# Edge aggregation of a graph layer: landing buffers filled one stage earlier, and remainder columns formed on VectorE

## The reference

```python
xl = (x @ Wl).reshape(n, H, D)
xr = (x @ Wr).reshape(n, H, D)
msg = xl[src] + xr[dst]
act = jnp.where(msg > 0, msg, NEG_SLOPE * msg)
e = jnp.einsum('ehd,hd->eh', act, att)
m = jax.ops.segment_max(e, dst, num_segments=n)
p = jnp.exp(e - m[dst])
denom = jax.ops.segment_sum(p, dst, num_segments=n)
alpha = p / (denom[dst] + 1e-16)
out = jax.ops.segment_sum(alpha[..., None] * xl[src], dst, num_segments=n)
return out.reshape(n, HID) @ W_up
```

## Time and profile before

| | |
|---|---|
| median of 3 runs | 1188.15 us (1183.03 to 1191.4) |
| the profiled execution | 1185.71 us, its span 1184.0 us |
| VectorE busy | 906.6 us (77%) |
| TensorE busy | 984.3 us (83%) |
| ScalarE busy | 603.7 us (51%) |
| GpSimd busy | 398.1 us (34%) |
| maxima / first seven groups / rest of aggregation / finish | from 603.9 / 652.7 / 686.0 / 921.6 us |

### The profile page before, as it was taken

How to read it: one execution, slowest core, us unless ns; L and a number is a source line. 1 busy time by engine, 2 the same in 40 slices (tenths; PEclk the granted TensorE clock), 3 DMA queues, 4 the chain that set the end, 5 groups by cost and what they waited for, 6 DMA issues and landing times. The chain is left out here.

```text
span 1184.0 us, 16374 instructions
## 1 busy us (share of the span) xinstructions
PE 984.3 (83%) x5021; PEld 793.5 (67%) x5021; DVE 906.6 (77%) x1499; ACT 603.7 (51%) x1356; POOL 398.1 (34%) x393
## 2 busy tenths in 40 slices
PE   0588399999999999999954779999997889999934
PEld 0475289999999999999931567777776344444412
DVE  3698177877888887887775679999995399887892
ACT  0243256665766666666633367777765224323411
POOL 0211477777777677777501000000001000000000
PEclk9899599999999999999988889999998899999966
DMA  4489588898898888888731776777764223422222
GB/s 150 120 208 154 165 250 265 279 263 262 243 296 269 272 249 263 276 260 263 236 107 53 251 237 207 242 235 211 222 200 140 65 92 93 98 70 72 50 35 35
DMA packets 106320, 220.76 MB, mean 186 GB/s; under 512 B 22658, under 2 KB 55003, under 8 KB 106127
## 3 DMA queue, kind: packets, MB, share of 16 engines
q1 hardware_dynamic: 83503, 152.48, 38.9%
q0 software_dynamic: 19904, 56.35, 21.7%
q10 hardware_dynamic: 2832, 10.89, 3.1%
HBM read 157.22 MB, written 73.01 MB: 194 GB/s over the span
## 5 line engine op out<-in xcount | busy, mean ns | idle before, releaser
L880 POOL DMA_INDIRECT score_gath<-xl_rows,misc x324 | 345.6, 1067 | 108.4 <-issue 95.5
L920 PE MATMUL score_ps_m<-x_hi,score_w_hi 128*128 128x416 f32 (+1 forms) x576 | 208.8, 362 | 0.4 <-DVE score_w_lo L1073 0.4
L1535 PE MATMUL agg_ps_o<-agg_gath,agg_hot 128*125 128x256 f32 x648 | 186.2, 424 | 24.6 <-DVE agg_hot L1651 24.1
L921 PE MATMUL score_ps_m<-x_lo,score_w_hi 128*128 128x416 f32 (+1 forms) x576 | 204.1, 354 | 0.0
L922 PE MATMUL score_ps_m<-x_hi,score_w_lo 128*128 128x416 f32 (+1 forms) x576 | 203.6, 353 | 0.0
L1594 ACT ACTIVATE agg_gath<-agg_gath,prob 128x64 f32<-128x64 f32 x648 | 158.4, 338 | 26.5 <-DMA agg_gath<-edge_rows 26.5
L1054 DVE TENSOR_TENSOR score_zb<-score_gath,score_ps_x 128x1024 f32<-128x1024 f32 x81 | 98.7, 1219 | 74.1 <-PE score_ps_x L903 71.6
L1535 PEld LDWEIGHTS agg_ps_o<-agg_gath,agg_hot 128*125 128x125 f32 x648 | 100.3, 192 | 59.5 <-issue 51.9
L975 ACT ACTIVATE score_mask_t<-score_local_bc,score_neg_iota 125x512 fp32r<-125x512 bf16 x81 | 58.3, 719 | 122.9 <-DMA score_local_bc<-local_rows 122.9
L903 PE MATMUL score_ps_x<-parts,score_mask_t 125*128 x648 | 93.8, 288 | 32.6 <-ACT score_mask_t L977 32.4
L1537 PE MATMUL agg_ps_o<-ext,agg_hot 128*125 128x18 f32 x324 | 118.8, 367 | 0.0
(11 more groups left out here) (320 smaller groups left out, 1654.6 us busy)
## 6 DMA issues: line engine op xcount, KB each, us to landing
edge_rows<-score_gath SPq DMA_DIRECT2D x81, 520.0 KB, 4.1
agg_gath<-edge_rows SPq DMA_DIRECT2D x81, 520.0 KB, 3.7
score_local_bc<-local_rows SPq DMA_DIRECT2D x40, 250.0 KB
score_gath<-xl_rows,misc POOLq DMA_INDIRECT x324, 4.6
x_rows<-in_x SPq DMA_DIRECT2D x10, 500.0 KB
xb_rows<-in_x ACTq DMA_DIRECT2D x1, 5000.0 KB, 21.2
xb_rows<-in_L_mix_bo POOLq DMA_DIRECT2D x1, 5000.0 KB, 42.8
phi_c<-phi_rows SPq DMA_DIRECT2D x10, 500.0 KB, 3.9
```

The costliest lines, as they stand in the source:

```text
L880: nc.gpsimd.indirect_dma_start(out=gath[:, g % GS, q, :], out_offset=None, in_=xl_rows, in_offset=bass.IndirectOffsetOnAxis(ap=src_idx[:, ...
L920: pe.matmul(acc, w_hi[:, i % 2, kk, :], x_hi[:, kk, cols], start=(kk == 0), stop=False)
L921: pe.matmul(acc, w_hi[:, i % 2, kk, :], x_lo[:, kk, cols], start=False, stop=False)
L1535: pe.matmul(o_flat[0:C, ds(cs[q] * HID, HID)], lhs.bitcast(F32), gath[:, g % GS, q, 0:HID], start=False, stop=False, skip_group_check=True)
```

## The change

`agg_gath` and its six semaphores are allocated before the maxima and live on into the aggregation. SP issues the loads of groups 0 to 5 at the start of the maxima, and in the aggregation starts with pair 0. To make room, `rows`, `on` and `cond` of the maxima lie in the memory of `parts`, beneath `ext`, which is written after they have been read for the last time. At the end of the maxima VectorE forms all three differences and signals ScalarE, then the three masked maxima, their rounded columns and their remainders; when ScalarE's rounded `prob` is there it forms that remainder too. GpSimd takes no part.

```diff
+AGG_SLOTS = 6
+def edge_load(sp, k, g):
+    sp.dma_start(k.agg_gath[:, g % AGG_SLOTS, :, :].rearrange("p q d -> p (q d)"), k.edge_rows[g, :, :]
+                 ).then_inc(k.s_load[g % AGG_SLOTS], 16)
...
 def maxima(nc, a, k):
...
-        rows = sb("rows", [HEADS, 4, PB * P])
-        on = sb("on", [HEADS, 3, PB * P])
-        cond = sb("cond", [HEADS, 6, PB * P])
+        in_parts = lambda name, n, at: nc.alloc_sbuf_tensor_at("max_" + name, [HEADS, n, PB * P], F32, offset=k.parts_at + 4 * PB * P * at)
+        rows, on, cond = in_parts("rows", 4, 0), in_parts("on", 3, 4), in_parts("cond", 6, 7)
...
             @block.sync
             def _(sp):
-                sp.wait_ge(s_pad, 1)
+                for g in range(AGG_SLOTS):
+                    edge_load(sp, k, g)
...
-                pool.wait_ge(s_exp, 1)
-                nc.gpsimd.tensor_tensor(k.ext[:, :, 9:9 + HEADS], k.prob[:, 0:NPAIR, :], k.ext[:, :, 0:HEADS].bitcast(F32), ALU.subtract)
-                pool.wait_ge(s_exp, 2)
-                nc.gpsimd.tensor_tensor(k.ext[:, :, 9 + HEADS:9 + 2 * HEADS], top_last[:, 0:NPAIR, :],
-                                        k.ext[:, :, HEADS:2 * HEADS].bitcast(F32), ALU.subtract)
...
-                act.activation(k.ext[:, :, HEADS:2 * HEADS], top_last[:, 0:NPAIR, :], ACT.Copy).then_inc(s_exp, 1)
-                act.wait_ge(s_exp, 2)
+                act.wait_ge(s_exp, 1)
...
                     q.mark(v.tensor_tensor(diff[:, pairs, :], k.score[:, pairs, :], m, ALU.subtract))
+                q.wait()
+                v.sem_inc(s_diff, 1)
+                for b in range(PB):
+                    m = ps_a[:, b, :].rearrange("p (h i) -> p i h", h=HEADS)
+                    pairs = slice(b * P, (b + 1) * P)
                     q.mark(v.tensor_tensor(top_last[:, pairs, :], m,
                                            last[:, pairs].unsqueeze(2).to_broadcast([P, P, HEADS]), ALU.mult))
                 q.wait()
-                v.sem_inc(s_diff, 1)
+                q.do(v.tensor_copy(k.ext[:, :, HEADS:2 * HEADS], top_last[:, 0:NPAIR, :]))
+                q.mark(v.tensor_tensor(k.ext[:, :, 9 + HEADS:9 + 2 * HEADS], top_last[:, 0:NPAIR, :],
+                                       k.ext[:, :, HEADS:2 * HEADS].bitcast(F32), ALU.subtract))
                 q.mark(v.tensor_copy(k.ext[:, :, 2 * HEADS], last[:, 0:NPAIR]))
-                q.do(v.tensor_scalar(k.ext[:, :, EXTW - 1], last[:, 0:NPAIR], 0.0, None, ALU.mult))
+                q.mark(v.tensor_scalar(k.ext[:, :, EXTW - 1], last[:, 0:NPAIR], 0.0, None, ALU.mult))
+                v.wait_ge(s_exp, 1)
+                q.do(v.tensor_tensor(k.ext[:, :, 9:9 + HEADS], k.prob[:, 0:NPAIR, :], k.ext[:, :, 0:HEADS].bitcast(F32), ALU.subtract))
...
 def aggregate(nc, a, k):
...
-                for g in range(2):
-                    load_edges(g)
                 load_pair(0)
-                load_edges(2)
-                load_edges(3)
                 load_phi(0)
                 load_phi(1)
                 for c in (3, 4):
                     sp.dma_start(phi_o[:, c - 3, :, :], k.phi_rows[0:3, :, C * c:C * c + C].rearrange("k p n -> p k n")).then_inc(s_phi_o, 16)
-                for g in range(4, GS):
-                    load_edges(g)
                 load_pair(1)
```

More of the change, by code:

```diff
@@ L116, in allocate @@
     parts = k.parts = sb("parts", [P, width])
+    k.parts_at = at(parts, 4 * width)
     k.ext = nc.alloc_sbuf_tensor_at("ext", [P, NPAIR, EXTW], F32R, offset=at(parts, 4 * width))
@@ L139, in allocate_late @@
 def allocate_late(nc, ctx, k):
+    k.s_load = [ctx.enter_context(nc.semaphore(f"s_load{i}")) for i in range(AGG_SLOTS)]
+    k.agg_gath = ctx.enter_context(nc.sbuf_tensor("agg_gath", [P, AGG_SLOTS, GP, XW], F32))
     k.prob = ctx.enter_context(nc.sbuf_tensor("prob", [P, PB * P, HEADS], F32))
@@ L1375, in aggregate @@
     NW = 3 * NJ
-    GS, OS = 6, 4
+    GS, OS = AGG_SLOTS, 4
     DQ = 2
@@ L1393, in sem @@
             return ctx.enter_context(nc.semaphore("agg_" + name))
-        gath = sb("gath", [P, GS, GP, XW])
+        gath = k.agg_gath
         hot = sb("hot", [P, OS, GP, C], F32R)
@@ L1418, in aggregate @@
         phi_of = lambda c: k.phi_c[:, c % 2, :, :] if c < 3 else phi_o[:, c - 3, :, :]
-        s_load = [sem(f"s_load{i}") for i in range(GS)]
+        s_load = k.s_load
         s_own_in = sem("s_own_in")
@@ L1446, in load_edges @@
                 def load_edges(g):
-                    if g >= GS:
-                        sp.wait_ge(s_agg, g - GS + 1)
-                    sp.dma_start(gath[:, g % GS, :, :].rearrange("p q d -> p (q d)"), k.edge_rows[g, :, :]).then_inc(s_load[g % GS], 16)
+                    sp.wait_ge(s_agg, g - GS + 1)
+                    edge_load(sp, k, g)
                 def load_phi(c):
```

## The result

The change took the median from 1187.07 us (22 runs, 1181.11 to 1196.84) to 1184.69 us (22 runs, 1179.24 to 1192.38). The ratio is 0.9958, with an interval of 0.9938 to 0.9978, which is 5.0 us (2.6 to 7.4) of the time before. The profiled execution took 1185.29 us, its span is 1183.6 us, only 0.4 us under the span before, and why that is so little is half of what follows.

What follows compares the result with a forecast made beforehand. VectorE's pace was taken to bound the aggregation, its start delayed by group 6 held behind own_rows. Terms 3.6 + 7.9 - 1.8 = 9.7 us gave 1178.5 us; range 1171 to 1186, the forecast's own 1175.7 to 1181.7.

Steps and rivals of the forecast that it cites:

- B: Rival, maxima: all six group loads go ahead of Wo, step 0 waits 7.9 us; 3.6 us gained, 1184.6 us; chance 0.11.
- C: Rival, aggregation start: phi issues set own_rows' start, only 3.0 us earlier; 4.8 us gained, 1183.4 us; chance 0.14.
- (a): End of the maxima: differences first, ScalarE's exponential starts at 641.8 instead of 643.6; 3.6 us together with (b).
- (b): End of the maxima: subtractions on VectorE, GpSimd's part and wait leave the path; block ends 3.6 us earlier.
- (c): Aggregation start: six group loads leave the queue ahead of own_rows, group 6 lands earlier; 7.9 us gained.
- (e): Buffers moved into parts, SP's dropped wait and its queue in the maxima: no cost.
- (d): Front of the maxima: six loads delay Wo tiles, 1.3 us at step 0 plus 0.5 at step 4; 1.8 us lost.
- The alternation: Maxima: SP's group loads and ScalarE's Wo loads take turns, one group beside the first Wo tile, 1.3 us more.
- And all behind it by the same amount: Aggregation and after: VectorE starting group 6 earlier moves the body and everything behind it by the same amount.
- A: Rival, aggregation start: own_rows no longer holds group 6, 12.7 instead of 7.9 us; 1173.7 us; chance 0.17.
- a 10 us issue behind own_rows: Sign, aggregation start: in the profile after, an issue behind own_rows still holds SP near 10 us.
- D: Rival, maxima: the six loads hold ScalarE at two Wo issues, 21.0 us; 9.5 us slower, 1197.7 us; chance 0.04.

Runs made afterwards that it cites:

- e3: Kernel before with only the end of the maxima changed, loads as before; 1189.99 us, ratio 0.9967.
- e1: Changed kernel plus one tiny GpSimd iota behind the reduction in the maxima; 1184.19 us, ratio 0.9924.
- e6: Changed kernel plus the early GpSimd iota and each of the six group loads behind its Wo tile; 1182.55 us, ratio 0.9916.
- e4: Kernel before with only the six group loads moved into the maxima, end of the maxima as before; 1188.32 us, ratio 0.9953.
- e8: e6 plus own_rows loaded in ten pieces behind later group loads; 1178.03 us (6 runs), ratio 0.9869.
- e12: e8 plus five overwritten TensorE transposes behind each of steps 0 to 4 of the Wo products; 1181.08 us, ratio 0.9890.
- e2: Changed kernel with each of the six group loads waiting for the Wo tile of the same number; 1182.86 us, ratio 0.9915.
- e9: Kernel before, unchanged, profiled a second time; 1187.70 us.
- e5: Changed kernel plus nine overwritten TensorE transposes between the transposes of the scores and step 0 of the Wo products; 1182.78 us, ratio 0.9916.
- e11: Kernel before, unchanged, profiled a third time; 1185.28 us.
- e7: Kernel before with own_rows loaded in ten pieces, one behind every sixth group load from group 7 on; 1182.65 us, ratio 0.9930.
- e10: Changed kernel, unchanged, profiled a second time; 1178.03 us.

## Why the prediction was right, and where it was wrong

The time, 1184.69 us, lies in the range of 1171 to 1186, and within 1% of before, which had the largest chance; but the forecast was 9.7 us of gain and the measurement 5.0. The forecast's own range, 1175.7 to 1181.7, missed it. The range held because it had been widened for B and C, whose times (1184.6 and 1183.4) are nearest to the measured one and whose mechanisms did not occur: the mechanisms were mostly right, and that the total stayed inside is in part luck. The terms in turn:

- **(a), (b), the end of the maxima:** forecast 3.6, measured 3.9 (13.42 to 9.51 us; e3 gives 3.87). The exponential starts 2.49 us behind the last copy (649.09 - 646.60), 1.8 earlier than before, as forecast. The subtractions take 1.59 and 1.60 us where 1.50 stood. The copy of 1296 elements takes 0.84 us: the lower bound, which I did not take. The two-elements-a-cycle rule of the Trainium skill (VectorE: DVE Perf Modes, section "The perf-mode tier table") holds for it, and the 0.47 us of the 324-element copy, from which I concluded against it, was no fair witness: that copy writes one column of 18 and the new one four side by side. Whether this is what makes it slower, no run tried. With the fast copy the term would have been 4.2, above what came, in part since the two long subtractions took 0.2 us more than was put down for them.

- **(c), six loads off the front of the queue:** forecast 7.9 us. Wherever GpSimd is on time it came out so: group 6 at T + 25.28 (e1), 25.55 (e6) and 25.75 (e4) for a forecast of 25.4, with waits of 4.54, 4.88 and 4.64 us for 4.8. In the change itself it is T + 27.12, 6.2 us gained. The term was right and another step took 1.8 us of it. One reading in it failed there: SP could issue group 6 not by T + 13.0 but at T + 16.09, when TensorE was through with the late group 0. The data still came by T + 24.12, and it was VectorE that came last.

- **(e), "no cost", and in (b) "GpSimd's part goes from the path with its wait":** this is the step that failed. The edit took away the instructions in which GpSimd changed over from the reduction, and with them the place where this change-over was hidden (a wait of 34.26 us in the earlier trace rows). It moved to the next ordinary instruction of the engine, the iota on which the whole aggregation starts. e1 shows it by giving the change-over another place, and e3 that it costs nothing as long as the data is later still. The Trainium skill (GPSIMD Engine Reference, section "Instruction dispatch") speaks of some 6 us to load the code at the first call of a freshly loaded kernel; the rows show 7.54 us ahead of the reduction before. Another 7.5 to 8.1 us behind it, on the way back, are in the rows of e1, e6, e8 and e12.

- **(d), the loads beside Wo:** forecast 1.3 us at step 0 and 1.8 at the stage's front. Step 0 came 1.5 us later (5.19, 5.29, 5.23 and 5.18 against 3.68), and e2 and e6 bring it back to 3.61 and 3.75, so the cause is shown. The loss to the stage is 1.2 us between the change and e9 (last copy at 42.87 and 41.68), but the change's step 0 was still at the full clock and 0.96 us shorter. Where step 0 is at the low clock on both sides the loss is 2.0 and 2.1 us (e1 and e4 against e9), near the 1.8. The third tile was not waited for there, since steps 2.8 us apart leave it the time; in e5, at full clock, step 4 waited 2.24 us for it. The alternation that I assumed, and that the Trainium skill states (DMA: Bandwidth & Descriptors, section "Queues, rings and completion order"), fits the 1.5 us; B, all six groups ahead of Wo, would have been 7.9.

- **Not in the prediction: the clock of the Wo steps.** It took the earlier trace rows for a property of the kernel. It is one of two levels, which differ between executions of the same program (before and e11, against e9) and are worth 6.25 us. Of eight profiles in which step 0 had its tile on time four had the low level (e2, e6, e7, e9), of the four with a late tile and no filling all four (after, e1, e4, e10). The length of step 0 tells two cases apart. In e1, e2, e4, e6, e7 and e9 it is 2.07 or 2.08 us: the clock, at 0.50 to 0.59 in the second half of the transposes ahead in all fourteen profiles, had not risen yet. In the others without filling it had risen by the end of step 0. It then stayed up through step 4 where the tile was on time (before, e3, e8, e11), and was down in or by step 2 behind a wait of 2.00 and 2.11 us in the change (after, e10). Falls behind a wait for a tile are also in e5 (2.24 us) and e8 (1.00 us). This makes it likely that the late tile takes the full clock away where there was one, but with two profiles against four it is not shown.

- **"And all behind it by the same amount"** (of the body of the aggregation): true to the end of the aggregation (2.80 and 2.79 us), not beyond. From group 6 to the end the change, e2, e5 and e6 took 499.91 to 500.54 us, before and the other kernels 497.40 to 498.35. So some 2.4 us of the lead were lost in `finish`, where TensorE ran the same matmuls with the low clock in other places. Why in these kernels is open: e6 and e1 differ only in when the six loads are issued, and lie on different sides.

The sum, at the low level on both sides, from stage start to group 6: before 55.11 + 33.34 = 88.45 us (e9), after 52.38 + 27.12 = 79.50, 8.95 us gained for 9.7 forecast (+3.9, +6.2, -1.2). Against an execution of before at full clock (48.86 + 33.30 = 82.16) it is 2.7, the 2.8 that the two first profiles show. To the end of the span it is 6.7 and 0.3 us, with the loss in `finish`. The measured 5.0 (2.6 to 7.4) lies between these two, as a mixture of both levels in the runs of before would make it.

The timed runs have no timeline, but most have their mean granted clock. Of the 74 of before that stand beside the experiments, the 22 with 0.937 or more have a median of 1186.79 us (1183.24 to 1190.63) and the 52 below it one of 1195.33 (1189.70 to 1205.62). The 22 runs of the change have no such split: 1185.37 us for the 6 with 0.937 or more, 1184.52 for the other 16. So the times of before lie in two groups that go with TensorE's clock, and those of the change near the faster one. A different share of the two would also explain why the medians of before differ (1187.07 and near 1194). In which stage the clock of these runs differed is not known, and how much of the missing 4.7 us is due to it stays open. Between stage start and group 6, at like clock, 0.75 of it is settled (9.7 less 8.95).

**Of the rivals,** A had the right price for its condition: e8 removes own_rows' hold and group 6 stands at T + 20.94 for A's T + 20.6. In the change VectorE had no wait at group 6 either, the sign that was named for A, but by a way that nobody had listed: VectorE was late, and SP issued group 6 late, when own_rows was nearly through. The sign of a 10 us issue behind own_rows did not come (0.95 us at most). B and C did not occur (step 0 was 1.5 us late, and own_rows was issued at T + 5.35). D did not either: ScalarE's next Wo issue, at 612.91, took 0.33 us. That own_rows is what makes the slow stretch, named as a point on which the prediction could be wrong, is shown by e7. The DMA view of the change between 670 and 676 us has the end of the stretch in its row of busy tenths:

```profile
DMA  3333333333333333333338889897989998549779
```

For half of the window 0.3 of the engines work, some 5 of 16; the Trainium skill (DMA: Bandwidth & Descriptors, section "Why a DMA increments its semaphore by 16 and not by 1") has a transfer to 125 partitions run on as many engines as the largest divisor up to 16, which is 5, and the row agrees.

## What to carry to other kernels

When the last use of an engine ahead of a barrier is removed, look in the program's order at what that use hid, such as the change-over behind a GpSimd library operation; give it a small instruction of its own in a place where nobody waits. When a queue stands still, find the transfer that runs over few engines and put it, in pieces, behind what is wanted first: here that one edit brought group 6 forward by 10.4 us, moving six loads a stage ahead by 7.6 (33.30 to 25.75 in e4). Timed they gained 8.4 and 5.6 us, which the intervals do not tell apart. And profile the unchanged kernel more than once before a stretch's clock is taken for given, and follow a lead to the end of the program before it is counted.

## What the runs showed of the hardware that was not expected

- Behind a `partition_all_reduce` the next ordinary GpSimd instruction waited for issue 7.48, 8.08, 7.88 and 7.70 us in the maxima (e1, e6, e8, e12), and came 8.32 to 8.42 and 9.61 us behind T in the aggregation (after, e2, e5, e10; e3), although GpSimd had had nothing else to do for over 30 us. The reduction itself waits for issue 7.4 to 7.5 us with little DMA traffic beside it (before, e3) and 9.2 to 10.0 with the six loads beside it (e1, e5, after, e10, e4).
- TensorE's granted clock in one and the same stretch of a program is 1.2 or 2.4 GHz from one execution to the next (before and e11 against e9): a step of two matmuls takes 1.10 us in every 1.9, or 2.04 in every 2.8.
- VectorE's rounding copy takes 0.84 us for 1296 elements where it writes four of 18 columns and 0.47 us for 324 where it writes one, that is 0.65 and 1.45 ns an element with the fixed part of an instruction in both.
- The load behind a transfer to 125 partitions was issued for 10.51 us (before; 11.88 in e9, 7.13 in e1), while a third of the DMA engines worked. Issued 10.4 us behind it (after) it was not held.
